# Error and update as one run of matmuls each in a delta-rule attention stage, gram moved between the value products and the error

## The chip, the cores and the metric

The kernel runs on one core of a Trainium2 chip. The metric is the device time of one execution in microseconds, the median of several runs. PE is TensorE, DVE VectorE, ACT ScalarE, POOL GpSimd, and SP the engine that issues the DMAs.

## The reference

Input x has 4 sequences of 4096 rows of 512 numbers; 16 heads of 32. The first layer is a delta rule, step after step in time, and the second a quantised projection:

```python
x = layernorm(x); v = x @ Wv.T; gate = sigmoid(x @ Wg.T); beta = sigmoid(x @ Wb.T)
rk = x by heads, each of norm 1;  wk = rk one row later
for each t:  err = (v_t - wk_t S) * beta_t
             S = S + wk_t err^T
             o_t = (rk_t S) * gate_t
x1  = x  + layernorm(o @ Wo.T)
out = x1 + layernorm(ffn(layernorm(x1)))    # ternary weight, inputs clipped to 128 levels
```

## The kernel before, in words

Three blocks run one after the other: `setup` (weights), `attention` (first layer, some 1850 us) and `feed_forward`. The change touches `attention` alone.

`attention` takes time in tiles of 32 rows of each of the 4 sequences, so 128 partitions and 128 tiles. The recurrence inside a tile is written as a triangular system per head, and tiles are chained by the state. The work is a software pipeline: step j handles tile j in the recurrence, tile j+7 in the value and key products (LAG_V), tile j+6 in the gram matrix (LAG_GRAM), tile j+9 in the turn of x (LAG_TURN), tile j+10 in the normalisation (LAG_XHAT), tile j-3 in the output product (LAG_Y), and so on. All is unrolled: there is no planner, each engine's function `step` has its instructions in an order written by hand, and each engine runs in that order, waiting on semaphores.

One step of PE, in the order before, with the helper that issues it:
- predict (`predict`, L949): the keys times the state, 16 matmuls with 32 weight columns, written as 32 by the hardware (fp32 takes two passes). ACT copies the result into rhs (L611), `turn_back` (L956) transposes it back, and DVE subtracts it from val into rhs (L831).
- value (`value`, L925 through `project`): 12 matmuls of 128x512 into ps_v for tile j+7. WHOLE is 12 and SHARE 3, and `value(first, end)` issues a part of the 12; the parts stand between the other groups.
- gram (L981), behind `gram_ready` (the keys in kbd, loaded by DMA): 16 matmuls, 32 in the hardware.
- error (`solve_error`, L962): 64 matmuls of 32x32 on the 16 small tiles of the array, 128 in the hardware, in two halves of 32 (64). `error_ready` waits for rhs (rhs_done) and for the solved system (tt_done).
- turn of x (L1003, 8) and keys (L1011, 4); ACT copies err (L688), xt and kt.
- output (`output`, L925): 12 matmuls of 128x512 into ps_y for tile j-3, again in parts.
- update (`update`, L1024): 64 matmuls of 32x32, 128 in the hardware, in two halves, behind `update_ready` (err_done, keyb_done). ACT copies the new state (L709), which predict of the next step needs.
- output turn (L1048, 8, behind POOL's olo_done) and gates (`project` with wgb, L925, 12 small ones, behind kt_done). `chain_ready` lets the next predict start.

DVE solves the systems: 30 columns for each pair of tiles (L800 and L808), spread over the steps by `solve(base, j, part)`. In every even step it also turns the systems of a pair (L752) before rhs, and at the end of every odd step it turns the solution back (L816). ss_raw (L838) is the sum of squares for the norms. POOL and ACT do the normalisations, masks and copies.

```python
value(SHARE + 3, 3 * SHARE - 1)
error_ready(base, j)
value(3 * SHARE - 1, 3 * SHARE)
solve_error(0)
last = value(3 * SHARE, 4 * SHARE)
if v_live:
    last.then_inc(s["v_psum"], 1)
last = solve_error(1)
```

Of the kernel before, what the change touches and what calls it, by code (L numbers as in the profile page):

```python
# [272 lines left out]
def attention(nc, io, k):  # L273
    with ExitStack() as ctx:
# [197 lines left out]
        def _(pool):  # L472
# [5 lines left out]
            def step(base, j):  # L478
# [54 lines left out]
                n, l, live = on(base, j, LAG_XHAT)  # L533
                if live:
                    wait(pool, s["xhat_done"], n + 1)
                    wait(pool, s["xhi_done"], n + 1)
                    wait(pool, s["xt_psum"], n - 1)
                    pool.tensor_tensor(x_part[:, l % 2, 1, :], x_hat[:, l % 4, :], x_part[:, l % 2, 0, :],  # L538
                                       ALU.subtract).then_inc(s["xlo_done"], 1)

                n, l, live = on(base, j, LAG_Z)
                if live:
# [8 lines left out]
                    pool.tensor_tensor(kept[:, 1:2], z_mean[:, l % 4, 0:1], kept[:, 0:1], ALU.mult).then_inc(s["z_scale"], 1)  # L551

# [13 lines left out]
                n, l, live = on(base, j, LAG_GRAM)  # L566
                if live:
                    wait(pool, s["gram_done"], n + 1)
                    wait(pool, s["bmask_done"], n + 1)
                    wait(pool, s["sys_done"], times(base, BODY // 2, (j + LAG_GRAM) // 2))  # L570
                    pool.tensor_tensor(m_t[:, :, l % 2, :], gram[:, :, :], b_mask[:, :, :], ALU.mult).then_inc(s["mt_done"], 1)  # L571

                n, l, live = on(base, j, LAG_PART)
                if live:
                    wait(pool, s["ohi_done"], n + 1)
                    wait(pool, s["ot_psum"], n - 1)
                    pool.tensor_tensor(o_part[:, l % 2, 1, :], o_g[:, :], o_part[:, l % 2, 0, :],  # L577
                                       ALU.subtract).then_inc(s["olo_done"], 1)

                n, l, live = on(base, j, 0)  # L580
                if live:
                    wait(pool, s["err_done"], n + 1)
                    wait(pool, s["v_done"], n + 1)
                    wait(pool, s["o_done"], n)
                    pool.tensor_tensor(pred[:, :], val[:, l, :], err[:, l % 2, :], ALU.subtract).then_inc(s["pred_done"], 1)  # L585
# [9 lines left out]
        def _(act):  # L595
            def step(base, j):

                n, l, live = on(base, j, LAG_STATS)
                if live:
                    act.wait_ge(x_loaded[l % 4], quads(base, j, LAG_STATS) * 16 + 16)  # L600
                    wait(act, s["ln_sums"], n)
                    wait(act, s["z_var"], upto(j - 1 + LAG_STATS2 + 1))
                    wait(act, s["ln_mean"], n - 1)
                    nc.scalar.activation(unread["ln", "sum"][:, :], x_in[:, l % 4, :], ACT.Copy,
                                         accum_out=ln_sum[:, l % 2:l % 2 + 1]).then_inc(s["ln_sums"], 1)
# [8 lines left out]
                if live:  # L614
# [5 lines left out]
                                         accum_out=y_var[:, l % 2:l % 2 + 1]).then_inc(s["y_var"], 1)  # L620
                n, l, live = on(base, j, LAG_STATS2)
# [17 lines left out]
                if live:  # L639
# [7 lines left out]
                    wait(act, s["xt_psum"], n - 1)  # L647
# [6 lines left out]
                n, l, live = on(base, j, LAG_PART)  # L654
                if live:
                    wait(act, s["o_done"], n + 1)
                    wait(act, s["ot_psum"], n - 1)
                    nc.scalar.activation(o_part[:, l % 2, 0, :], o_g[:, :], ACT.Copy).then_inc(s["ohi_done"], 1)

                n, l, live = on(base, j, LAG_NORM)  # L660
                if live:
                    wait(act, s["ss_done"], n + 1)
                    wait(act, s["rn0_done"], n)
                    nc.scalar.activation(ss_ln[:, :], ss[:, l % 2, :], ACT.Ln, scale=float(2 ** LN_SHIFT)).then_inc(s["ln_done"], 1)
                    wait(act, s["ln_done"], n + 1)
                    wait(act, s["rn_done"], n - 1)
                    nc.scalar.activation(rn0[:, l % 2, :], ss_ln[:, :], ACT.Exp, scale=-0.5,
# [690 lines left out]
```

## Time and profile before

| what | value |
|---|---|
| median of 3 runs | 2324.56 us (2321.91 to 2326.44) |
| span of the profiled execution | 2313.7 us |
| PE matmul busy | 2084.1 us, 90%, 50216 matmuls and as many weight loads |
| DVE busy | 1992.1 us, 86% |
| ACT busy | 1774.0 us, 77% |
| POOL busy | 1729.0 us, 75% |
| queue "instruction" on q8 | 397 packets, 6.50 MB |

The profile gives the span from the first to the last instruction; it gives no time of its own for the whole execution, and the median of the runs lies 10.9 us above the span. Rows of a timeline give start, duration, engine, line, operation, output and inputs, and in brackets the idle time of the engine before the row with what released it; "issue" is time in which the engine waited for nothing that the profile shows. Matmuls overlap, so the cost of a group is read from its start to the start of the next group. TensorE's granted clock is full speed throughout the loop.

### The profile page before, as it was taken

How to read it: one execution, taken by the hardware profiler on the slowest of the kernel's cores; microseconds unless marked ns; L12 is line 12 of the kernel's file. 1: busy time of each engine (PE TensorE's matmuls, PEld its weight loads, DVE VectorE, ACT ScalarE, POOL GpSimd, SP SyncE). 2: the span in 40 equal slices, each digit the busy share in tenths (PEclk: the TensorE clock that was granted, in tenths of full speed). 3: DMA queues.
4: the chain of work that ended last, by engine and by line, in shares of the span. 5: the costliest groups of instructions: out<-in, count | busy, mean ns of one | idle time of the engine just before them, and what ended most of it. 6: DMA issues, size and time to landing. Idle time of an engine off the chain costs nothing. (4 is left out here: it accounts for less than half of the span.)

```text
span 2313.7 us, 123730 instructions
## 1 busy us (share of the span) xinstructions
PE 2084.1 (90%) x50216; PEld 1316.0 (57%) x50216; DVE 1992.1 (86%) x5810; ACT 1774.0 (77%) x3756; POOL 1729.0 (75%) x3099
## 2 busy tenths in 40 slices
PE   1679999999999999999999999999999987499997
PEld 1346666666666666666655656566666654255554
DVE  5388999999999999999889999899999994588886
ACT  3667888888888888888877878788888744477775
POOL 2668888888888888888888888888888854244443
PEclk7789999999999999999999999999999988799999
DMA  2122333333333333333333333333333222488885
GB/s 86 48 65 80 98 100 98 98 98 95 99 97 99 94 94 95 95 94 94 93 91 93 94 96 91 94 97 96 100 96 99 82 78 67 150 225 229 225 231 129
DMA packets 156632, 247.69 MB, mean 107 GB/s; under 512 B 39544, under 2 KB 39552, under 8 KB 156064
## 3 DMA queue, kind: packets, MB, share of 16 engines
q1 hardware_dynamic: 156064, 239.78, 36.6%
q8 instruction: 397, 6.50, 1.2%
q14 instruction: 171, 1.40, 0.2%
HBM read 104.40 MB, written 67.11 MB: 74 GB/s over the span
## 5 line engine op out<-in xcount | busy, mean ns | idle before, releaser
L800 DVE TENSOR_TENSOR ps_elim<-ps_elim,sys 128x30 f32<-128x30 f32 (+14 forms) x1920 | 543.3, 326 | 0.7
L808 DVE TENSOR_TENSOR sys<-sys,ps_elim 128x30 f32<-128x30 f32 (+14 forms) x1920 | 534.6, 316 | 1.0
L925 PE MATMUL ps_v<-wv,xt 128*128 128x512 f16 x1536 | 435.2, 389 | 39.6 <-DVE rhs L831 16.5
L925 PE MATMUL ps_y<-wo,ot 128*128 128x512 f16 x1536 | 406.1, 386 | 17.3 <-DVE x L852 9.5
L962 PEld LDWEIGHTS ps_chain<-rhs,t_t 32*32 32x32 f32 x16384 | 257.3, 144 | 110.6 <-issue 110.5
L962 PE MATMUL ps_chain<-rhs,t_t 32*32 32x32 f32 x16384 | 286.1, 218 | 13.9 <-issue 8.5
L709 ACT ACTIVATE state<-ps_s 128x512 f32<-128x512 f32 x128 | 76.5, 598 | 265.6 <-PE ps_s L1024 263.6
L1024 PEld LDWEIGHTS ps_s<-err,key_b 32*32 32x32 f32 x16384 | 172.1, 106 | 147.4 <-issue 147.2
L1310 PE MATMUL ps_f<-wq,f_xq 128*128 128x512 f16 x1024 | 242.5, 381 | 6.8 <-DVE f_xq L1276 6.8
L538 POOL TENSOR_TENSOR x_part<-x_hat,x_part 128x512 f16<-128x512 f32 x128 | 148.7, 1162 | 131.6 <-ACT x_hat L645 111.5
L1024 PE MATMUL ps_s<-err,key_b 32*32 32x32 f32 x16384 | 205.5, 195 | 34.2 <-issue 34.2
L925 PEld LDWEIGHTS ps_v<-wv,xt 128*128 128x128 f16 x1536 | 121.0, 99 | 188.4 <-issue 120.5
L925 PEld LDWEIGHTS ps_y<-wo,ot 128*128 128x128 f16 x1536 | 130.2, 98 | 130.3 <-issue 26.3
L831 DVE TENSOR_TENSOR rhs<-val,ps_chain 128x512 f32<-128x512 f32 x128 | 87.4, 682 | 121.1 <-PE ps_chain L956 121.1
L1158 POOL TENSOR_TENSOR f_y_veps<-f_y_var,y_eps 128x1 f32<-128x1 f32 x128 | 53.6, 418 | 184.3 <-ACT f_unread L1191 183.4
L585 POOL TENSOR_TENSOR pred<-val,err 128x512 f32<-128x512 f32 x128 | 163.1, 1274 | 11.3 <-ACT err L688 11.2
L571 POOL TENSOR_TENSOR m_t<-gram,b_mask 128x512 f32<-128x512 f32 x128 | 163.5, 1277 | 5.3 <-ACT gram L674 5.2
L512 POOL TENSOR_TENSOR b_mask<-gates,neg_mask 128x512 f32<-128x512 f32 x128 | 135.5, 1059 | 32.0 <-DVE gates L879 31.9
L1310 PEld LDWEIGHTS ps_f<-wq,f_xq 128*128 128x128 f16 x1024 | 100.2, 98 | 102.0 <-DVE f_xq L1276 7.5
L577 POOL TENSOR_TENSOR o_part<-o_g,o_part 128x512 f16<-128x512 f32 x128 | 148.5, 1160 | 0.0
L949 PE MATMUL ps_chain<-key_bd,state 128*32 128x128 f32 x4096 | 139.9, 277 | 4.3 <-issue 2.8
L714 ACT ACTIVATE ot<-ps_gram 128x1024 f16<-128x1024 f16 x128 | 130.9, 1022 | 16.8 <-PE ps_gram L1048 16.7
(163 smaller groups left out, 5123.6 us busy)
## 6 DMA issues: line engine op xcount, KB each, us to landing
x_in<-in_L_attn_x SPq DMA_DIRECT2D x128, 256.0 KB
kbd<-kt SPq DMA_DIRECT2D x512, 64.0 KB, 2.1
key_bd<-key_t SPq DMA_DIRECT2D x512, 64.0 KB, 2.4
x_res<-in_L_attn_x SPq DMA_DIRECT2D x128, 256.0 KB
x_scratch<-x SPq DMA_DIRECT2D x128, 256.0 KB, 6.3
f_x<-x_scratch SPq DMA_DIRECT2D x32, 1024.0 KB, 7.6
out<-f_res SPq DMA_DIRECT2D x128, 256.0 KB, 3.9
gate<-gates SPq DMA_DIRECT2D x128, 7.9 KB
```

Source lines behind the costliest of these rows:

```text
L512: pool.tensor_tensor(b_mask[:, :, :], beta.unsqueeze(1).to_broadcast([P, C, H]), k["neg_mask"][:, :].unsqueeze(2).to_broadcast([P, C, H]), ...
L538: pool.tensor_tensor(x_part[:, l % 2, 1, :], x_hat[:, l % 4, :], x_part[:, l % 2, 0, :], ALU.subtract).then_inc(s["xlo_done"], 1)
L571: pool.tensor_tensor(m_t[:, :, l % 2, :], gram[:, :, :], b_mask[:, :, :], ALU.mult).then_inc(s["mt_done"], 1)
L577: pool.tensor_tensor(o_part[:, l % 2, 1, :], o_g[:, :], o_part[:, l % 2, 0, :], ALU.subtract).then_inc(s["olo_done"], 1)
L585: pool.tensor_tensor(pred[:, :], val[:, l, :], err[:, l % 2, :], ALU.subtract).then_inc(s["pred_done"], 1)
L800: dve.tensor_tensor(tmp, factors(r, c, first, end)[:, c - first:C - 1 - first, c - first:c - first + 1].to_broadcast(shape), sys[:, r, c:c ...
L808: dve.tensor_tensor(dst, dst, tmp, ALU.add).then_inc(elim_done[r], 1)
L925: last = pe.matmul(out, lhs[:, a, kb, :], weights[:, w, kb, :], start=(i == 0), stop=(i == 3 * KB - 1))
L949: last = pe.matmul(out, state[:, l % 2, HD * h:HD * h + HD], key_bd[:, :, h, :], start=True, stop=True)
L962: last = pe.matmul(ps_chain[q, e], t_t[q, l // 2 % 2, :, l % 2, h], rhs[q, e], start=True, stop=True)
L1024: last = pe.matmul(ps_s[q, e], key_b[q, l, e], err[q, l % 2, e], start=(isinstance(n, int) and n == 0 and h == 0), stop=True, skip_group_c ...
L1310: last = pe.matmul(ps_f[i][:, :], xq[:, r % 2, a, kb, P * i:P * i + P], k["wq"][:, kb, :], start=(m == 0), stop=(m == 2 * KB - 1))
```

## The change

Nothing is computed otherwise; the orders of four engines change.

- PE: all 12 value matmuls are issued before gram (4 before `turn_back`, 8 behind it). `gram_ready` and `error_ready` stand together before gram, so gram comes behind the wait for rhs, and the error's two halves follow it with nothing between. The update's two halves follow each other as well. Five output matmuls stand before the update (three before), then three, the gates, four, and the output turn is last.
- DVE: the reduction ss_raw stands before rhs.
- ACT: the copy of the turned prediction and the square of ps_y come before the sum over x_in; val and gram come before x_part and x_sq; o_part, ss_ln and rn0 come after kt; z before the gates, and ot last.
- POOL: the scale of z comes before x_part; m_t, pred and o_part follow x_part; rn comes after them, and o_g last.

```diff
@@ -823,6 +828,11 @@
                 systems(base, j)
                 diagonal(base, j)
                 multipliers(base, j)
+                m, k_l, k_live = on(base, j, LAG_TURN)
+                if k_live:
+                    wait(dve, s["sq_done"], m + 1)
+                    wait(dve, s["ss_done"], m)
+                    dve.tensor_reduce(ss_raw[:, :], heads(x_sq[:, k_l % 2, :]), AX_X, ALU.add).then_inc(s["ss_sum"], 1)
                 n, l, live = on(base, j, 0)
                 if live:
                     wait(dve, s["pred_psum"], n + 1)
@@ -831,11 +841,6 @@
                     dve.tensor_tensor(rhs[:, :], val[:, l, :], ps_chain[:, :], ALU.subtract).then_inc(s["rhs_done"], 1)
                 solve(base, j, 0)
 
-                m, k_l, k_live = on(base, j, LAG_TURN)
-                if k_live:
-                    wait(dve, s["sq_done"], m + 1)
-                    wait(dve, s["ss_done"], m)
-                    dve.tensor_reduce(ss_raw[:, :], heads(x_sq[:, k_l % 2, :]), AX_X, ALU.add).then_inc(s["ss_sum"], 1)
                 if k_live:
                     wait(dve, s["ss_sum"], m + 1)
                     wait(dve, s["ln_done"], m - 1)
@@ -970,9 +975,11 @@
                     wait(pe, s["xt_done"], upto(v + 2))
                 value(0, SHARE + 1)
                 turn_back()
-                value(SHARE + 1, SHARE + 2)
+                last = value(SHARE + 1, WHOLE)
+                if v_live:
+                    last.then_inc(s["v_psum"], 1)
                 gram_ready(base, j)
-                value(SHARE + 2, SHARE + 3)
+                error_ready(base, j)
                 if m_live:
                     for g in range(KB):
                         for b in range(B):
@@ -980,13 +987,7 @@
                             out = ps_gram[q, :].rearrange("p (i h) -> p h i", h=H)[:, HB * g:HB * g + HB, :]
                             last = pe.matmul(out, kt[:, m_l % 2, g, q], kbd[:, m_l % 2, :, g, q], start=True, stop=True)
                     last.then_inc(s["gram_psum"], 1)
-                value(SHARE + 3, 3 * SHARE - 1)
-                error_ready(base, j)
-                value(3 * SHARE - 1, 3 * SHARE)
                 solve_error(0)
-                last = value(3 * SHARE, 4 * SHARE)
-                if v_live:
-                    last.then_inc(s["v_psum"], 1)
                 last = solve_error(1)
                 if live:
                     last.then_inc(s["err_psum"], 1)
@@ -1028,14 +1029,21 @@
                 if y_live:
                     wait(pe, s["x1_done"], y)
                     wait(pe, s["ot_done"], y + 1)
-                output(0, SHARE - 1)
+                output(0, SHARE + 1)
                 update_ready(base, j)
-                output(SHARE - 1, SHARE)
+                output(SHARE + 1, SHARE + 2)
                 update(0)
-                output(SHARE, 2 * SHARE)
                 last = update(1)
                 if live:
                     last.then_inc(s["s_psum"], 1)
+                output(SHARE + 2, 2 * SHARE + 2)
+
+                if v_live:
+                    wait(pe, s["kt_done"], v + 1)
+                    project(ps_g[:, 0:2 * H], xt[:, v_l % 4], k["wgb"], range(WHOLE)).then_inc(s["g_psum"], 1)
+                last = output(2 * SHARE + 2, WHOLE)
+                if y_live:
+                    last.then_inc(s["y_psum"], 1)
 
                 n, l, live = on(base, j, LAG_OUT)
                 if live:
@@ -1049,16 +1057,8 @@
                                                 o_part[:, l % 2, a, P * kb:P * kb + P], k["ident_half"][:, :])
                     last.then_inc(s["ot_psum"], 1)
 
-                if v_live:
-                    wait(pe, s["kt_done"], v + 1)
-                    project(ps_g[:, 0:2 * H], xt[:, v_l % 4], k["wgb"], range(WHOLE)).then_inc(s["g_psum"], 1)
-
-                output(2 * SHARE, WHOLE - 1)
                 if y_live:
                     chain_ready(base, j + 1)
-                last = output(WHOLE - 1, WHOLE)
-                if y_live:
-                    last.then_inc(s["y_psum"], 1)
             run(step)
 
```

Of ACT's part, the pieces that move between x_hat and err:

```diff
@@ -644,12 +646,50 @@
                     sc = ln_sc[:, l % 2, :]
                     nc.scalar.activation(x_hat[:, l % 4, :], x_in[:, l % 4, :], ACT.Identity,
                                          scale=sc[:, 0:1], bias=sc[:, 1:2]).then_inc(s["xhat_done"], 1)
+                n, l, live = on(base, j, LAG_V)
+                if live:
+                    wait(act, s["v_psum"], n + 1)
+                    wait(act, s["o_done"], n - 7)
+                    wait(act, s["rhs_done"], n - 7)
+                    nc.scalar.activation(val[:, l, :], ps_v[:, :], ACT.Copy).then_inc(s["v_done"], 1)
+
+                n, l, live = on(base, j, LAG_GRAM)
+                if live:
+                    wait(act, s["gram_psum"], n + 1)
+                    wait(act, s["mt_done"], n)
+                    nc.scalar.activation(gram[:, :, :].rearrange("p i h -> p (i h)"), ps_gram[:, :], ACT.Copy).then_inc(s["gram_done"], 1)
+
+                n, l, live = on(base, j, LAG_XHAT)
...
                     wait(act, s["xt_psum"], n - 1)
                     nc.scalar.activation(x_part[:, l % 2, 0, :], x_in[:, l % 4, :], ACT.Identity,
                                          scale=sc[:, 0:1], bias=sc[:, 1:2]).then_inc(s["xhi_done"], 1)
                     wait(act, s["ss_sum"], n - 1)
                     nc.scalar.activation(x_sq[:, l % 2, :], x_in[:, l % 4, :], ACT.Square,
                                          scale=sc[:, 0:1], bias=sc[:, 1:2]).then_inc(s["sq_done"], 1)
+
+                n, l, live = on(base, j, 0)
+                if live:
+                    wait(act, s["err_psum"], n + 1)
+                    wait(act, s["s_psum"], n - 1)
+                    wait(act, s["pred_done"], n - 1)
+                    nc.scalar.activation(err[:, l % 2, :], ps_chain[:, :], ACT.Copy).then_inc(s["err_done"], 1)
+
+                n, l, live = on(base, j, LAG_TURN)
+                if live:
+                    wait(act, s["xt_psum"], n + 1)
+                    wait(act, s["g_psum"], n - 3)
+                    last, most, src = later(l)
+                    nc.scalar.activation(last, src[:, :, 0:1], ACT.Copy)
+                    nc.scalar.activation(most, src[:, :, 1:C], ACT.Copy).then_inc(s["xt_done"], 1)
...
```

PE, one step in the middle of the loop, before (a row is a group of equal matmuls, "x16" their number as written; of the fp32 ones the hardware runs two for each):

```order
L949 MATMUL ps_chain<-key_bd,state 32x128 x16
L925 MATMUL ps_v<-wv,xt 128x512 x4
L956 MATMUL ps_chain<-ident,rhs 128x128 x4
L925 MATMUL ps_v<-wv,xt 128x512 x2
L981 MATMUL ps_gram<-kbd,kt 32x4x32 x16
L925 MATMUL ps_v<-wv,xt 128x512 x3
L962 MATMUL ps_chain<-rhs,t_t 32x32 x32
L925 MATMUL ps_v<-wv,xt 128x512 x3
L962 MATMUL ps_chain<-rhs,t_t 32x32 x32
L1003 MATMUL ps_gram<-ident_half,x_part 128x128 x8
L1011 MATMUL ps_v<-ident,key 128x128 x4
L925 MATMUL ps_y<-wo,ot 128x512 x3
```

The same stretch in the changed kernel, from predict on:

```order
L954 MATMUL ps_chain<-key_bd,state 32x128 x16
L930 MATMUL ps_v<-wv,xt 128x512 x4
L961 MATMUL ps_chain<-ident,rhs 128x128 x4
L930 MATMUL ps_v<-wv,xt 128x512 x8
L988 MATMUL ps_gram<-kbd,kt 32x4x32 x16
L967 MATMUL ps_chain<-rhs,t_t 32x32 x64
L1004 MATMUL ps_gram<-ident_half,x_part 128x128 x8
L1012 MATMUL ps_v<-ident,key 128x128 x4
L930 MATMUL ps_y<-wo,ot 128x512 x5
L1025 MATMUL ps_s<-err,key_b 32x32 x64
```

The error is one row of 64 where it was two of 32 with value matmuls between, gram stands directly before it, and the update is one row.

PE again, the end of the step before the change (from the second half of the update):

```order
L1024 MATMUL ps_s<-err,key_b 32x32 x32
L925 MATMUL ps_y<-wo,ot 128x512 x3
L1024 MATMUL ps_s<-err,key_b 32x32 x32
L1048 MATMUL ps_gram<-ident_half,o_part 128x128 x8
L925 MATMUL ps_v<-wgb,xt 128x32 x12
L925 MATMUL ps_y<-wo,ot 128x512 x6
```

and in the changed kernel, from the update:

```order
L1025 MATMUL ps_s<-err,key_b 32x32 x64
L930 MATMUL ps_y<-wo,ot 128x512 x3
L930 MATMUL ps_v<-wgb,xt 128x32 x12
L930 MATMUL ps_y<-wo,ot 128x512 x4
L1056 MATMUL ps_gram<-ident_half,o_part 128x128 x8
L954 MATMUL ps_chain<-key_bd,state 32x128 x16
```

The output turn (L1048, now L1056) has gone behind the gates and the last four output matmuls, directly before the next predict.

DVE at the start of an even step, before:

```order
L752 STREAM_TRANSPOSE sys<-m_t 128x1024
L759 MEMSET sys 128x32
L779 COPY ps_elim<-sys 128x105
L779 COPY ps_elim<-sys 128x210
L831 TENSOR_TENSOR rhs<-val,ps_chain 128x512
L800 TENSOR_TENSOR ps_elim<-ps_elim,sys 128x240
L800 TENSOR_TENSOR ps_elim<-ps_elim,sys 128x30
...
L808 TENSOR_TENSOR sys<-sys,ps_elim 128x29x2
L838 TENSOR_REDUCE ss_raw<-x_sq 128x16
L843 TENSOR_SCALAR ss<-ss_raw 128x16
```

and now:

```order
L757 STREAM_TRANSPOSE sys<-m_t 128x1024
L764 MEMSET sys 128x32
L784 COPY ps_elim<-sys 128x105
L784 COPY ps_elim<-sys 128x210
L835 TENSOR_REDUCE ss_raw<-x_sq 128x16
L841 TENSOR_TENSOR rhs<-val,ps_chain 128x512
L805 TENSOR_TENSOR ps_elim<-ps_elim,sys 128x240
...
L813 TENSOR_TENSOR sys<-sys,ps_elim 128x29x2
L848 TENSOR_SCALAR ss<-ss_raw 128x16
```

ss_raw (L838, now L835) has moved from behind the first part of the elimination to the place before rhs.

## Rows read from the trace of the kernel before

**Rows 1.** The page, busy time, share of the span and instructions of each engine

```profile
PE 2084.1 (90%) x50216; PEld 1316.0 (57%) x50216; DVE 1992.1 (86%) x5810; ACT 1774.0 (77%) x3756; POOL 1729.0 (75%) x3099
```

**Rows 2.** Timeline of DVE, 386 to 421 us: start, duration, operation, [idle before]

```profile
391.81 0.68 DVE L831 TENSOR_TENSOR rhs<-val,ps_chain 128x512 f32<-128x512 f32 x1
...
404.36 0.69 DVE L831 TENSOR_TENSOR rhs<-val,ps_chain 128x512 f32<-128x512 f32 x1 [1.23 <-PE ps_chain L956]
...
419.70 0.68 DVE L831 TENSOR_TENSOR rhs<-val,ps_chain 128x512 f32<-128x512 f32 x1
```

**Rows 3.** Timeline of PE, predict of two steps, 116 steps apart

```profile
193.17 1.08 PE L949 MATMUL ps_chain<-key_bd,state 128*32 128x128 f32 x32
...
1856.26 1.08 PE L949 MATMUL ps_chain<-key_bd,state 128*32 128x128 f32 x32
```

**Rows 4.** Timeline of PE, 1012 to 1032 us, around two updates

```profile
1012.28 0.63 PE L1011 MATMUL ps_v<-ident,key 128*128 128x128 f32 x4
...
1014.92 0.65 PE L1024 MATMUL ps_s<-err,key_b 32*32 32x32 f32 x52
1016.44 0.31 PE L1024 MATMUL ps_s<-err,key_b 32*32 32x32 f32 x12 [0.86 <-issue]
...
1031.33 0.32 PE L1024 MATMUL ps_s<-err,key_b 32*32 32x32 f32 x13 [1.16 <-issue]
```

**Rows 5.** The page, DMA queue, kind: packets, MB, share of 16 engines

```profile
q8 instruction: 397, 6.50, 1.2%
```

**Rows 6.** Timeline of PE, 1170 to 1182 and 1233 to 1239 us

```profile
1170.70 1.11 PE L962 MATMUL ps_chain<-rhs,t_t 32*32 32x32 f32 x64
...
1173.98 0.30 PE L962 MATMUL ps_chain<-rhs,t_t 32*32 32x32 f32 x3 [0.39 <-issue]
...
1178.95 0.39 PE L1024 MATMUL ps_s<-err,key_b 32*32 32x32 f32 x23 [1.10 <-issue]
...
1234.15 0.31 PE L962 MATMUL ps_chain<-rhs,t_t 32*32 32x32 f32 x7 [0.45 <-issue]
...
1238.61 0.44 PE L1024 MATMUL ps_s<-err,key_b 32*32 32x32 f32 x27 [0.61 <-issue]
```

**Rows 7.** Two stretches: us, busy of PE, PEld, DVE, ACT, POOL, clock, DMA

```profile
200.00:480.00 280.00, 274.41 (x7662) 177.77 (x7656) 261.87 (x848) 239.60 (x520) 248.87 (x441) 1.00 0.34 97
500.00:1130.00 630.00, 597.56 (x16553) 387.35 (x16551) 575.65 (x1848) 522.11 (x1137) 541.13 (x958) 1.00 0.33 96
```

**Rows 8.** Timeline of PE, an even step without a stop on "issue", 390 to 402 us

```profile
390.70 1.08 PE L981 MATMUL ps_gram<-kbd,kt 128*32 128x128 f32 x32
391.72 0.60 PE L925 MATMUL ps_v<-wv,xt 128*128 128x512 f16 x2
392.63 0.38 PE L925 MATMUL ps_v<-wv,xt 128*128 128x512 f16 x1 [0.31 <-DVE rhs L831]
392.94 1.11 PE L962 MATMUL ps_chain<-rhs,t_t 32*32 32x32 f32 x64
393.98 0.82 PE L925 MATMUL ps_v<-wv,xt 128*128 128x512 f16 x3
...
395.78 0.62 PE L1003 MATMUL ps_gram<-ident_half,x_part 128*128 128x128 f16 x8
...
396.68 0.81 PE L925 MATMUL ps_y<-wo,ot 128*128 128x512 f16 x3
...
398.12 0.82 PE L925 MATMUL ps_y<-wo,ot 128*128 128x512 f16 x3
398.88 0.75 PE L1024 MATMUL ps_s<-err,key_b 32*32 32x32 f32 x64
399.62 0.61 PE L1048 MATMUL ps_gram<-ident_half,o_part 128*128 128x128 f16 x8
...
400.36 1.45 PE L925 MATMUL ps_y<-wo,ot 128*128 128x512 f16 x6
401.75 1.08 PE L949 MATMUL ps_chain<-key_bd,state 128*32 128x128 f32 x32
```

More of the change, by code:

```diff
@@ L531, in step @@
                     pool.tensor_tensor(sc[:, 0:1], sc[:, 2:3], k["neg_half"][:, :], ALU.pow).then_inc(s["y_rstd"], 1)
[L533 to L539, printed above, removed]
                 n, l, live = on(base, j, LAG_Z)
@@ L551, in step @@
                     pool.tensor_tensor(kept[:, 1:2], z_mean[:, l % 4, 0:1], kept[:, 0:1], ALU.mult).then_inc(s["z_scale"], 1)
+                n, l, live = on(base, j, LAG_XHAT)
+                if live:
+                    wait(pool, s["xhat_done"], n + 1)
+                    wait(pool, s["xhi_done"], n + 1)
+                    wait(pool, s["xt_psum"], n - 1)
+                    pool.tensor_tensor(x_part[:, l % 2, 1, :], x_hat[:, l % 4, :], x_part[:, l % 2, 0, :],
+                                       ALU.subtract).then_inc(s["xlo_done"], 1)
+                n, l, live = on(base, j, LAG_GRAM)
+                if live:
+                    wait(pool, s["gram_done"], n + 1)
+                    wait(pool, s["bmask_done"], n + 1)
+                    wait(pool, s["sys_done"], times(base, BODY // 2, (j + LAG_GRAM) // 2))
+                    pool.tensor_tensor(m_t[:, :, l % 2, :], gram[:, :, :], b_mask[:, :, :], ALU.mult).then_inc(s["mt_done"], 1)
+                n, l, live = on(base, j, 0)
+                if live:
+                    wait(pool, s["err_done"], n + 1)
+                    wait(pool, s["v_done"], n + 1)
+                    wait(pool, s["o_done"], n)
+                    pool.tensor_tensor(pred[:, :], val[:, l, :], err[:, l % 2, :], ALU.subtract).then_inc(s["pred_done"], 1)
+                n, l, live = on(base, j, LAG_PART)
+                if live:
+                    wait(pool, s["ohi_done"], n + 1)
+                    wait(pool, s["ot_psum"], n - 1)
+                    pool.tensor_tensor(o_part[:, l % 2, 1, :], o_g[:, :], o_part[:, l % 2, 0, :],
+                                       ALU.subtract).then_inc(s["olo_done"], 1)
                 n, l, live = on(base, j, LAG_NORM)
@@ L564, in step @@
                     pool.tensor_tensor(rn[:, l % 2, :], t[:, 2, :], y, ALU.mult).then_inc(s["rn_done"], 1)
[L566 to L578, printed above, removed]
                 n, l, live = on(base, j, 0)
                 if live:
[L582 to L585, printed above, removed]
                     wait(pool, s["pred_done"], n + 1)
@@ L596, in step @@
             def step(base, j):
[L598 to L605, printed above, removed]
                 n, l, live = on(base, j, 0)
@@ L620, in step @@
                                          accum_out=y_var[:, l % 2:l % 2 + 1]).then_inc(s["y_var"], 1)
+                n, l, live = on(base, j, LAG_STATS)
+                if live:
+                    act.wait_ge(x_loaded[l % 4], quads(base, j, LAG_STATS) * 16 + 16)
+                    wait(act, s["ln_sums"], n)
+                    wait(act, s["z_var"], upto(j - 1 + LAG_STATS2 + 1))
+                    wait(act, s["ln_mean"], n - 1)
+                    nc.scalar.activation(unread["ln", "sum"][:, :], x_in[:, l % 4, :], ACT.Copy,
+                                         accum_out=ln_sum[:, l % 2:l % 2 + 1]).then_inc(s["ln_sums"], 1)
                 n, l, live = on(base, j, LAG_STATS2)
```

71 lines of the change are left out of this document (33 added, 38 removed).

## Prediction, made before the changed kernel ran

> **What bounds the kernel now.** I read the engines' busy shares first, then DVE's timeline, then PE's, then the DMA queues. PE is busy 90% and DVE 86% of the span [rows 1]; neither is far from full. DVE waits for rhs in every second step, so the unit is a pair of steps, and DVE's timeline gives its two halves [rows 2]. From rhs of an even step (391.81) to rhs of the odd one (404.36) is 12.55 us, and DVE sat idle 1.23 us before the latter: PE sets this half A. From 404.36 to the next even rhs (419.70) is 15.34 us, and that rhs had no idle time before it: DVE, with its two big transposes, sets this half B. A clean pair is 27.89 us, 13.95 a step. The mean over 116 steps is longer: predict groups start at 193.17 and at 1856.26 [rows 3], 14.34 a step, 28.67 a pair. The missing 0.78 us a pair is what the next two paragraphs explain.
>
> In PE's rows a second kind of stop appears that no engine releases [rows 4]. The second half of the update breaks off after 52 matmuls and goes on at 1016.44 after 0.86 us of "issue"; one step later it goes on at 1031.33 with 13 instead of 12 matmuls left. A step has 380 matmuls (predict 32, value 12, turn back 4, gram 32, error 128, turn 8, keys 4, output 12, update 128, gates 12, output turn 8), as many weight loads and, by the code, some ten waits: about 770 instructions. The page's queue "instruction" on q8 moved 397 packets and 6.50 MB [rows 5], 16.4 KB a packet; with 2 x 50216 matmuls and loads [rows 1] that is 253 of them a packet, 256 with the waits. A step is then three blocks and two instructions, so a block's end comes one matmul earlier in the order each step, which is what 12 and then 13 left over show. I read these stops as PE waiting for its own instructions.
>
> The prices: two late blocks in a row resume at 1173.98 and 1178.95, and at 1234.15 and 1238.61 [rows 6], some 126 matmuls apart: a block takes 4.5 to 5.0 us, mean 4.7, after a late one. After a punctual one it takes less: the block that ends late at 1016.44 began 126 matmuls earlier, at the start of the keys' transposes at 1012.28 [rows 4], 4.2 us; the one that ends late at 1173.98 began just behind 1170.70 [rows 6], 3.3 us. Where instructions are long, nobody notices: in 200 to 480 us PE is busy 274.4 of 280 us, in 500 to 1130 us only 597.6 of 630 [rows 7], 2% idle against 5%, with the same work in each step and block ends at other places. The Trainium skill says the opposite (Runtime: NRT & Kernel Launch, section Instruction fetch mechanics): fetching in blocks of 256 instructions is hidden, because instructions issue slower than they are fetched. The rows above speak against it here. By the page these stops would be something else and need not grow; that outcome is the first rival.
>
> **The change, part by part.**
>
> *Fewer changes of matmul form.* Six output matmuls before predict take 1.39 us (400.36 to 401.75), three before an update 0.76 (398.12 to 398.88) [rows 8]: 0.21 each and 0.13 for going over to small tiles. Leaving them shows in no row by itself; I take 0.1 for a change either way, bounds 0 and 0.13. Before, a step enters and leaves small tiles six times; now three times (predict; gram and error together; update), with one change from gram's form to error's between. Five changes fewer are 0.5 us of PE a step (0.2 to 0.65). By that term alone the step would shrink from 14.34 to 13.84, 58 us in 116 steps, if PE were the only bound. The Trainium skill (TensorEngine Tiling (Array Packing), section Key Properties) has the rule behind it, that a change of tiling mode drains the engine; it speaks for the change, and what speaks against is below.
>
> *Half A.* PE's way from the start of the error (392.94) to the odd rhs (404.36) is 11.42 us [rows 2, 8]. Out of it go three value matmuls (0.64, now ahead of the gate for rhs) and four form changes (0.4); into it comes gram, which now stands behind that gate: 1.02 us (390.70 to 391.72) [rows 8]. That is 11.4. The value matmul and its wait between the end of rhs (391.81 + 0.68) and the error, 0.45, shrink to 0.1. A becomes 0.68 + 0.1 + 11.4 = 12.2, 0.35 less than 12.55.
>
> *Half B.* DVE's own instructions stay, so 15.34 stays. The reduction of squares (ss_raw) goes ahead of rhs in every step; what it adds before one rhs it takes away before the next, so it leaves each half as long as it was and costs nothing. If that cover were gone it would cost its own place in A, at most the idle 1.23. PE's way through half B is now some 13.0 us (11.42 from the error on, and 2.1 for two value matmuls, gram and three value matmuls before it, less 0.5), so late blocks of up to 2.3 us in B cost nothing; before it was 1.8.
>
> *Blocks of instructions.* This term decides. From the start of gram to the end of the update PE took 8.4 us (390.70 to 399.62, less half a us of wait for rhs) [rows 8] for 312 matmuls: 3.45 us per 128, one block. Now the same stretch holds gram 1.0, error 2.0 (two times 1.04 less one form change), turn and keys 0.9 (395.78 to 396.68), five output matmuls 1.2, update 1.4 (two times 0.74 less 0.1): 6.5 us for 305 matmuls, 2.7 us a block. The number of instructions stays. A block after a punctual one needs 3.3 to 4.2, so it is late by 0.6 to 1.5, and after a late one 4.7, so late by 2.0. Three block ends fall into the stretch in (305 - 256) / 128, 38% of the steps: together 0.6 and 2.0, 2.6. In the others two do: about 0.9, and some 0.5 for the block that runs on into the long matmuls behind. The mean is 0.38 x 2.6 + 0.62 x 1.4 = 1.85 us a step, against 0.78 now.
>
> *Waits on the other engines.* ACT copies val and gram ahead of x_part and x_sq, whose readers come a step later. The copy of err ends the chain gram, its copy, two passes, while PE spends 3.0 us on gram and error: even, and one more output matmul (0.2) stands before the update: 0. The state copy has output, gates and output turn as cover. POOL's o_part after pred is awaited only at the step's end. SP's queue is not touched; its loads of kbd and key_bd start when ACT's kt and DVE's key_t are done, as before. I take 0 for all of these, bounds -0.2 and +0.3 a pair.
>
> **The sum.** A: 12.2 + 1.85 = 14.05; B: 15.34. The pair is 29.4, before 28.67: +0.7, +0.35 a step, and with 116 steps +40 us. The loop's ends and the second stage stay. The span of the profiled execution would go from 2313.7 to some 2353; the median of the runs (2324.56) lies 11 us above that span, so it goes to about 2363, and I say 2362. If late time stays at 0.78 the pair is 28.3, 58 pairs are -20 us: 2304. If the stretch costs 3.5 us (first block 4.2) in 38% and 2.0 in the rest, the mean is 2.6 and the worst steps overflow B's cover of 2.3 by some 0.2 a pair: 30.3, +1.65 a pair, 2420; I cut that end at 2405.
>
> **Rivals.**
> 1. *The stops do not grow.* For: in 200 to 480 us there are nearly none, although PE is as full. Against: the remainder that grows by one, and stops of the same kind inside the error [rows 6]. Then -20 us, 2304, faster; it decides if late time stays under 0.78 + 0.35 us a step, what half A gains otherwise. Chance 0.20.
> 2. *DVE covers it.* If most late blocks fall into half B, late time in A of 1.15 gives 12.2 + 1.15 + 15.34 = 28.7 a pair, 2326, the same. Against: a block's end moves by one matmul a step, so both halves see it. Chance 0.05.
> 3. *The gate for rhs before gram.* In even steps rhs ends late; now gram, its copy, m_t and err queue behind it, not the error alone. If the copy of err comes 0.25 late each step a pair costs another 0.5: +29 on the forecast, 2391. For: two ACT passes stand between gram and err. Against: the two chains come out even. Chance 0.10.
>
> **How the numbers follow.** The forecast, slower by late blocks, has 0.65. About 0.2% (4.6 us) is what a measurement can tell from no change. Faster is rival 1, 0.20; the same is rival 2, 0.05; slower are the forecast and rival 3, 0.75. The range reaches from just under rival 1, 2298, to near the upper bound of late blocks, 2405.
>
> **What would show it.** Right: idle time of PE on "issue" in error, update, output and gates of over 1.5 us a step in most steps, its place moving by one matmul a step; no value matmul between the halves of the error and PE's busy time lower; clean pairs of some 27.5 us where they occur; more idle time of DVE before the odd rhs than 1.23 us. Wrong: pairs of 27.5 to 28.3 throughout (rival 1); idle time of PE that ACT's err releases (rival 3); "issue" stops whose place does not move.

## The result, and the profile after

Four runs of the changed kernel have a median of 2363.45 us (2355.82 to 2369.17), the kernel before 2325.5 beside them: a ratio of 1.0164, with a 95% interval of 1.0134 to 1.0194. It is slower by 1.6%, some 38 us. Forecast were 2362 us and "slower". The profiled execution took 2355.82 us, its span is 2354.1.

In this run and in all later ones the span lies 1.7 to 1.8 us below the time of the same execution. So a profile is one execution of several, and not always a typical one: the profiled one of before (span 2313.7) was some 9 us faster than the median of its kernel, this one 7.6 us faster. Traces are compared below with that in mind; what an edit is worth is read from the medians.

The page of the changed kernel, busy time of each engine, then the costliest groups that answer to the update, the error and gram (line, engine, operation, tiles, count | busy, mean ns | idle before, releaser):

```profile
PE 2036.5 (87%) x50216; PEld 1361.3 (58%) x50216; DVE 1955.2 (83%) x5810; ACT 1804.7 (77%) x3756; POOL 1724.8 (73%) x3099
...
L967 PE MATMUL ps_chain<-rhs,t_t 32*32 32x32 f32 x16384 | 268.8, 218 | 32.0 <-issue 26.7
...
L1025 PE MATMUL ps_s<-err,key_b 32*32 32x32 f32 x16384 | 195.7, 195 | 65.0 <-issue 64.4
...
L988 PE MATMUL ps_gram<-kbd,kt 128*32 128x128 f32 x4096 | 138.4, 275 | 42.9 <-DVE rhs L841 41.1
```

Against [rows 1] PE is busy 47.6 us less, with the same 50216 matmuls, and yet the kernel is slower. The last lines name two waits of PE that outweigh it: idle time on "issue" in update and error, and a wait for DVE's rhs ahead of gram.

Timeline of PE, predict of the two steps that [rows 3] shows of before:

```profile
188.87 1.12 PE L954 MATMUL ps_chain<-key_bd,state 128*32 128x128 f32 x32
...
1891.95 1.08 PE L954 MATMUL ps_chain<-key_bd,state 128*32 128x128 f32 x32
```

That is 1703.1 us for 116 steps, 14.68 a step against 14.34: 40 us more. All of the loss is in the loop.

Timeline of PE, two steps in a row, around the stops:

```profile
1018.71 0.22 PE L1004 MATMUL ps_gram<-ident_half,x_part 128*128 128x128 f16 x1 [0.42 <-issue]
...
1022.75 0.31 PE L1025 MATMUL ps_s<-err,key_b 32*32 32x32 f32 x11 [0.96 <-issue]
...
1033.85 0.27 PE L1004 MATMUL ps_gram<-ident_half,x_part 128*128 128x128 f16 x2 [0.66 <-issue]
...
1038.17 0.31 PE L1025 MATMUL ps_s<-err,key_b 32*32 32x32 f32 x12 [1.23 <-issue]
```

These are the stops of [rows 4]: 11 matmuls of the update left over, then 12; 1 transpose of the turn left over, then 2. The place moves by one matmul a step, and now there are two stops in a step. Between 193 and 1856 us PE's idle time on "issue" sums up to 107.2 us in the table of waits, against 47.1 before.

Timeline of DVE, rhs of an even step, of the odd one behind it and of the next even one, with the residual sum (L857) between:

```profile
303.24 0.68 DVE L841 TENSOR_TENSOR rhs<-val,ps_chain 128x512 f32<-128x512 f32 x1
...
315.69 0.69 DVE L841 TENSOR_TENSOR rhs<-val,ps_chain 128x512 f32<-128x512 f32 x1 [1.40 <-PE ps_chain L961]
320.15 0.75 DVE L857 SCALAR_TENSOR_TENSOR x<-ps_y,y_sc,x_res 128x512 f32<-128x512 f32 x1 [1.64 <-DMA x_res<-in_L_attn_x]
...
332.19 0.68 DVE L841 TENSOR_TENSOR rhs<-val,ps_chain 128x512 f32<-128x512 f32 x1
```

Half A is 12.45 us here (forecast without stops: 12.2), half B 16.50 (forecast: 15.34, as in [rows 2]). In this pair B has grown because DVE sat 1.64 us waiting for the load of x_res, for which it never waited this long before. Over the 58 pairs from step 4 on, by the starts of rhs, the mean of A went from 13.23 to 13.64 and that of B from 15.45 to 15.75.

Over the loop another wait of DVE grew more. Its `gates` row (the reciprocal near the end of a step) waits for ACT's g_den, which follows the gate matmuls of PE. Tables of waits from 193 to 1856 us, before, changed, and then a_locked and a_locked_late, two kernels of the next section that differ only in where blocks of PE's instructions end:

```profile
DVE gates L879 <- ACT g_den L724: 20.2, 28, 2.0
...
DVE gates L884 <- ACT g_den L732: 76.0, 69, 2.7
...
DVE gates L884 <- ACT g_den L732: 8.4, 19, 0.7
...
DVE gates L884 <- ACT g_den L732: 157.1, 107, 3.2
```

So late blocks reach DVE by this path as well as by rhs. Summed by halves over the 58 pairs, DVE's idle time went from 1.91 to 2.53 us a pair in A and from 0.13 to 0.90 in B. In A nearly all of the growth is g_den (17.2 to 49.4 us in 58 pairs); in B it is g_den (1.0 to 26.6) and, less, the row that reads x_res (6.5 to 24.2).

DVE's own work, on the other hand, became shorter: 1955.2 us busy against 1992.1, and by halves, idle time taken out, 11.11 us against 11.32 in A and 14.85 against 15.32 in B. Most of it is ss, which stood directly behind ss_raw and now stands behind a part of the elimination (groups of DVE, before and changed: busy, mean ns | idle before):

```profile
L843 DVE TENSOR_SCALAR ss<-ss_raw 128x16 f32<-128x16 f32 x128 | 50.0, 390 | 4.8 <-POOL rn_t L559 0.5
...
L848 DVE TENSOR_SCALAR ss<-ss_raw 128x16 f32<-128x16 f32 x128 | 22.7, 177 | 1.7 <-POOL rn_t L579 1.5
```

Why ss is the shorter there was not tried by itself.

Two timelines of the same moment: PE, and stretches of 3.4 us (us, PE busy, granted clock as a share of 2.4 GHz, DMA share, GB/s):

```profile
333.02 1.08 PE L988 MATMUL ps_gram<-kbd,kt 128*32 128x128 f32 x32 [2.28 <-DVE rhs L841]
334.03 2.04 PE L967 MATMUL ps_chain<-rhs,t_t 32*32 32x32 f32 x128
336.00 1.03 PE L1004 MATMUL ps_gram<-ident_half,x_part 128*128 128x128 f16 x8
336.83 1.05 PE L1012 MATMUL ps_v<-ident,key 128*128 128x128 f32 x4
```

```profile
327.50:330.90 3.40, 3.24 (x20) 1.00 0.50 110
330.90:334.30 3.40, 1.28 (x52) 1.00 0.24 90
334.30:337.70 3.40, 3.40 (x137) 0.50 0.27 90
```

PE waits 2.28 us ahead of gram, and 1.3 us behind that wait the clock falls to 1.2 GHz for 3.4 us. The error takes no longer in it, the transposes do: 1.03 and 1.05 us, where the clock is full 0.62 and 0.63. There are 15 such falls between 200 and 1850 us; before, there is none.

### The profile page after: what moved, and what is told of

It reads as the page before. It is cut to its first block and busy times, and to the rows that moved or that the text cites. A ratio compares the mean times of both kernels' runs of the same rounds, so it can differ in the third digit from the quotient of the medians.

```text
span 2354.1 us, 123730 instructions
## 1 busy us (share of the span) xinstructions
PE 2036.5 (87%) x50216; PEld 1361.3 (58%) x50216; DVE 1955.2 (83%) x5810; ACT 1804.7 (77%) x3756; POOL 1724.8 (73%) x3099
## 5 line engine op out<-in xcount | busy, mean ns | idle before, releaser
L930 PE MATMUL ps_y<-wo,ot 128*128 128x512 f16 x1536 | 413.7, 394 | 21.0 <-DVE x L857 11.2
L930 PE MATMUL ps_v<-wv,xt 128*128 128x512 f16 x1536 | 385.9, 390 | 6.5 <-ACT xt L685 4.2
L967 PE MATMUL ps_chain<-rhs,t_t 32*32 32x32 f32 x16384 | 268.8, 218 | 32.0 <-issue 26.7
L967 PEld LDWEIGHTS ps_chain<-rhs,t_t 32*32 32x32 f32 x16384 | 250.6, 145 | 61.3 <-issue 61.2
L1025 PE MATMUL ps_s<-err,key_b 32*32 32x32 f32 x16384 | 195.7, 195 | 65.0 <-issue 64.4
L930 PEld LDWEIGHTS ps_v<-wv,xt 128*128 128x128 f16 x1536 | 142.8, 100 | 164.4 <-issue 39.6
L988 PE MATMUL ps_gram<-kbd,kt 128*32 128x128 f32 x4096 | 138.4, 275 | 42.9 <-DVE rhs L841 41.1
L988 PEld LDWEIGHTS ps_gram<-kbd,kt 128*32 128x32 f32 x4096 | 105.8, 109 | 99.8 <-issue 99.8
```

Source lines behind the costliest of these rows:

```text
L930: last = pe.matmul(out, lhs[:, a, kb, :], weights[:, w, kb, :], start=(i == 0), stop=(i == 3 * KB - 1))
L967: last = pe.matmul(ps_chain[q, e], t_t[q, l // 2 % 2, :, l % 2, h], rhs[q, e], start=True, stop=True)
L988: last = pe.matmul(out, kt[:, m_l % 2, g, q], kbd[:, m_l % 2, :, g, q], start=True, stop=True)
L1025: last = pe.matmul(ps_s[q, e], key_b[q, l, e], err[q, l % 2, e], start=(isinstance(n, int) and n == 0 and h == 0), stop=True, skip_group_c ...
```

## The experiments

The open questions were: are the stops on "issue" really late blocks of instructions; are they the loss, or is it the wait for rhs ahead of gram (rival 3); and what stands behind them.

**Stops at fixed places.** A step is 770 instructions, three blocks and two: the traces of before and of the changed kernel have exactly 770 records of PE (matmuls, weight loads and its sequencer's) from one predict to the next. Two of PE's waits in it repeat what PE has already waited for, with the same value. Without them a step is 768 in the trace, and a block's end stays where it is.

```
-                    wait(pe, s["xt_done"], upto(v + 2))
+                    if not on(base, j - 1, LAG_OUT)[2]:
+                        wait(pe, s["xt_done"], upto(v + 2))
...
                     wait(pe, s["x1_done"], y)
-                    wait(pe, s["ot_done"], y + 1)
+                    if not on(base, j, LAG_GRAM)[2]:
+                        wait(pe, s["ot_done"], y + 1)
```

For the two "late" kernels this stands ahead of PE's first step as well; the traces have 1190 records of PE ahead of the first predict where the others have 1030, so 320 waits are 160 instructions:

```
+            for i in range(320):
+                pe.wait_ge(s["state_done"], 1)
```

> The kernel before, with two waits a step left out on PE that repeat a wait PE has already passed, so that a step is 768 instructions, three blocks of 256. If the stops are late blocks, a block's end stays at the places of steps 4 to 11 (in predict, in the error, in the update), where the trace of before shows 13.75 us a step and hardly a stop: 13.8 to 13.95 a step for 116 steps against 14.34, some 2262 to 2280 us, below both kernels. Rival, the stops are not tied to the count of instructions: they stay, two short waits fewer, 2315 to 2325.

> As b_locked, but 320 waits that are met at once stand ahead of PE's first step (160 instructions), which puts the block ends at the places of steps 80 to 92 (gram, middle of the error, middle of the update), for good. If the stops are late blocks: 14.65 us a step as the trace of before shows there, 2360 us, some 90 above b_locked with the same work. Rival: the same time as b_locked.

> The changed kernel with the same two repeated waits left out, block ends as in b_locked. If late blocks are the loss, nearly no stops: 13.65 us a step as in its own steps 4 to 11, up to 14.3 if what steps 12 to 20 show is the new wait for rhs ahead of gram: 2250 to 2320, I take 2296. Against b_locked it tells what the change does without late blocks: my first rival's arithmetic says 20 us less than b_locked; if the gate for rhs ahead of gram costs more than the form changes give, it is slower than b_locked. Rival (stops not tied to instructions): 2355.

> The changed kernel, locked as b_locked_late. If late blocks are the loss: 15.4 us a step as in its steps 76 to 90, against 14.68 on average, some 2445 us, and its distance to a_locked (150) is larger than that of the two before (90). Rival: the same time as a_locked.

Measured: b_locked 2311.1 us, ratio 0.9961 (0.9931 to 0.9992); b_locked_late 2355.8, 1.0140 (1.0121 to 1.0158); a_locked 2326.5, 0.9999 (0.9984 to 1.0014); a_locked_late 2427.4, 1.0443 (1.0423 to 1.0463).

Each pair has the same work in the same order on every engine and differs only by waits that are met at once, ahead of the loop; 45 us lie between the two of before and 101 between the two of the change. Two steps in a row of a_locked_late, timeline of PE:

```profile
871.43 0.42 PE L969 MATMUL ps_chain<-rhs,t_t 32*32 32x32 f32 x14 [0.58 <-issue]
...
876.24 0.46 PE L1028 MATMUL ps_s<-err,key_b 32*32 32x32 f32 x33 [1.38 <-issue]
...
890.64 0.46 PE L1028 MATMUL ps_s<-err,key_b 32*32 32x32 f32 x33 [1.11 <-issue]
```

33 matmuls are left over in both steps: the stop no longer moves. In a_locked and b_locked the stops on "issue" are gone (0.0 and 0.5 us between 193 and 1850). So the stops follow the count of PE's instructions, and the order of the change pays more for them.

The sizes were missed in both good cases: 2262 to 2280 was expected for b_locked, and a_locked was to be faster than it, not 15 us slower. In b_locked 47 us of stops are gone and only some 9 are won by the ratio (2 to 16 by its interval). Its table of waits from 193 to 1856 us (engine, line waited for: us, times, longest), PE first and then SP:

```profile
PE ps_v L925 <- DMA kbd<-kt: 56.0, 67, 1.4
...
PE ps_y L925 <- DMA key_bd<-key_t: 10.5, 34, 0.7
...
SPq L456 <- ACT kt L702: 7.8, 7, 3.1
SPq L440 <- DVE gates L879: 1.0, 3, 0.5
```

PE now waits for the loads of kbd and key_bd, for which it waited 4.1 and 4.7 us before, and SP, which issues them, waits for other engines 8.8 us in 1663. It has its next transfer to issue nearly all the time. Half A fell from 13.23 to 12.95, half B rose from 15.45 to 15.77. That the sum does not fall is the choice of executions: the profiled one of b_locked was 9 us slower than its median, the profiled one of before some 9 faster. In a_locked PE waits at the gate for rhs ahead of gram, and else it is the same in other places:

```profile
PE ps_gram L989 <- DVE rhs L841: 100.2, 56, 2.6
PE ps_chain L954 <- DMA key_bd<-key_t: 30.8, 54, 1.1
...
DVE x L857 <- DMA x_res<-in_L_attn_x: 63.9, 41, 2.4
DVE x L857 <- issue: 23.0, 30, 2.3
```

The row "issue" is very probably the same wait: its 30 cases start 6.3 to 7.2 us after SP issued x_res, the 41 named ones 6.1 to 7.6. Both together are 86.9 us in a_locked, 26.5 in b_locked, 29.1 in the changed kernel and 7.8 in before.

Like with like, without late blocks on either side, the change is still some 0.4% slower (0.9999 against 0.9961, 15 us; the two intervals just touch).

**SP's queue, and the wait for rhs.** In the "act" kernels the load of x_in is issued by ACT from step 0 on, with the same waits; in the "gate" kernels the wait for rhs stands behind gram:

```
-                gram_ready(base, j)
-                error_ready(base, j)
+                gram_ready(base, j)
                 if m_live:
...
+                error_ready(base, j)
                 solve_error(0)
```

> b_locked showed no late block, yet 14.35 us a step: PE waits there for the kbd loads (56 us in 67 waits) and SP's queue hardly ever waits for an engine (7.8 us in 1664). Theory: once late blocks are gone, SP's queue of 13 transfers a step is the bound. Here x_in is loaded from ACT's queue from step 0 on, nothing else differs from b_locked. By the theory the waits for kbd and x_res go and a step falls to the 13.8 to 14.0 that half A and half B allow: 2265 to 2285 us. Rival: the transfers themselves are late (DMA engines or memory), whatever the queue: 2305 to 2320.

> The changed kernel, locked, x_in loaded from ACT's queue. a_locked waits 63.9 us for x_res on DVE and 30.8 for key_bd on PE. If SP's queue is the cause both go: 2326 becomes 2280 to 2300. What then stays above b_locked_act is the price of the order itself, the gate for rhs ahead of gram. Rival: 2320 to 2330.

> The changed kernel, locked, with the wait for rhs put between gram and the error, not ahead of gram. a_locked has PE waiting 100 us ahead of gram in 56 even steps for DVE's rhs. Theory: gram's 1.0 us stands on the way from the even rhs to the odd one, so moving it ahead of the wait gives up to 1.0 us a pair, 58 us, cut by SP's queue which is at 14.3 us a step: 2290 to 2315. Rival, the wait for rhs only moves and the pair is set by DVE or SP alone: 2326 as a_locked.

> All three: locked, x_in from ACT's queue, the wait for rhs behind gram. If late blocks, SP's queue and the gate are the three losses of the change, what is left is the gain of fewer changes of form: half A 0.35 us or more below b_locked_act's, 20 us or more: 2240 to 2265. Rival: the form changes give nothing and it equals b_locked_act.

Measured: b_locked_act 2309.1, 0.9938 (0.9913 to 0.9963); a_locked_act 2307.7, 0.9939 (0.9913 to 0.9966); a_locked_gate 2309.2, 0.9924 (0.9894 to 0.9954); a_locked_gate_act 2272.9, 0.9778 (0.9734 to 0.9822).

The theory of SP's queue holds in half. PE's wait for kbd falls from 56.0 to 5.1 us in b_locked_act and the one for key_bd from 30.8 to 5.1 in a_locked_act, but DVE's for x_res stays, 26.3 and 54.9 (with "issue" 28.0, and 109.3 where a_locked had 86.9), and single ones become longer:

```profile
DVE x L859 <- DMA x_res<-in_L_attn_x: 26.3, 17, 3.9
```

That is b_locked_act; the longest was 1.2 us in b_locked. So b_locked gains too little to be told from nothing (the intervals overlap), not the 26 to 46 us expected, while a_locked gains 0.6%. Where DVE waits for it in b_locked_act, it goes on 8.5 us after the issue of x_res on average, in b_locked 6.8 us after. So at least that part lies behind the issue and not in SP's order; what holds the transfer up was not tried.

The gate was worth 0.75%, 17 us, as expected. Each of the two edits alone brings the locked kernel to 2308 or 2309, both together to 2273. The tables of waits show how one takes what the other frees. In a_locked PE waits 100.2 us for rhs and 30.8 for key_bd. With the gate edit these are 43.0 and 50.2; with the x_in edit 86.5 and 5.1; with both 40.7 and 2.0. That kernel is below both kernels of the case, 2.2% under before. Its page and the predict of the same two steps:

```profile
PE 2026.4 (89%) x50216; PEld 1353.9 (60%) x50216; DVE 1968.6 (87%) x5810; ACT 1799.6 (79%) x3756; POOL 1723.1 (76%) x3099
```

```profile
191.08 1.40 PE L961 MATMUL ps_chain<-key_bd,state 128*32 128x128 f32 x32
...
1811.70 1.08 PE L961 MATMUL ps_chain<-key_bd,state 128*32 128x128 f32 x32
```

13.97 a step: half A 12.09, half B 15.86. DVE's idle time ahead of rhs is 15.2 us in the 58 pairs, against 92.3 in before: PE hardly sets half A any more. DVE's wait at the row that reads x_res is still 88.6 us ("issue" counted in), the largest of DVE's that is left.

**The change itself, taken apart.** a_gate is the changed kernel with the gate edit alone, a_gate_act with the x_in edit too; both keep 770 instructions. The other two cross the kernels: PE's whole block from one, the rest of the program from the other.

> The changed kernel with only the wait for rhs moved from ahead of gram to ahead of the error; block ends move by one matmul a step as they did. In the locked kernels this was worth 17 us (2326 to 2309). Theory: late blocks are the larger part of the loss and stay, so about as much is won: 2340 to 2352, still slower than before. If the gate were the main cause of the loss, it would fall to 2325 or below.

> As a_locked_gate_act (2273), but not locked: the two repeated waits are back and a block's end moves by one matmul a step. Late blocks alone make the difference: the change lost 37 us between its locked and its plain form, so 2305 to 2320 here. If locking gave nothing beyond two waits fewer, 2275 to 2285.

> PE's order of the changed kernel, DVE, ACT and POOL in the order of before. If the loss lies in PE's order alone (my term of 0 for the other engines), 2355 to 2370 as the changed kernel. If the other engines' new order is what makes the change bearable, slower: 2380 and more. If it is part of the loss, faster than 2355.

> PE's order of before, DVE, ACT and POOL in the order of the change. If the other engines' order costs nothing: 2320 to 2332. If it costs, more; with late blocks as in before in any case.

Measured: a_gate 2323.7, 1.0003 (0.9977 to 1.0029); a_gate_act 2312.9, 0.9948 (0.9921 to 0.9974); pe_after_rest_before 2508.7, 1.0801 (1.0758 to 1.0844); pe_before_rest_after 2424.9, 1.0443 (1.0403 to 1.0483).

a_gate was expected at 2340 to 2352 and came out as before: one wait, moved by 32 matmuls, takes back the whole loss. Its timelines of PE and of DVE:

```profile
306.95 1.08 PE L987 MATMUL ps_gram<-kbd,kt 128*32 128x128 f32 x32
308.83 2.02 PE L967 MATMUL ps_chain<-rhs,t_t 32*32 32x32 f32 x128 [0.80 <-DVE rhs L841]
```

```profile
308.01 0.68 DVE L841 TENSOR_TENSOR rhs<-val,ps_chain 128x512 f32<-128x512 f32 x1
...
319.52 0.69 DVE L841 TENSOR_TENSOR rhs<-val,ps_chain 128x512 f32<-128x512 f32 x1
```

Gram runs while DVE computes rhs, and this half A is 11.51 us, 0.94 less than the 12.45 above, which is gram's 1.02. Half B grew there, and took back a part: by the means over the 58 pairs A is 12.89 and B 16.03. The falls of the clock are nearly as many (13), so they are not the difference. The stops on "issue" are fewer, 77.8 us against 107.2, still more than the 47.1 of before.

a_gate_act against a_locked_gate_act puts the price of late blocks at 1.7%, 40 us, in the middle of what was expected.

The crossed kernels are slower than either, by 8.0% and 4.4%, far outside what was expected of them (2355 to 2370, and 2320 to 2332). In pe_after_rest_before the table of PE's waits has among its first places:

```profile
PE ps_chain L956 <- ACT rhs L611: 113.4, 103, 1.3
...
PE ps_v L925 <- ACT g_exp L720: 27.5, 98, 0.3
```

ACT comes late with the copy that turning back needs, in nearly every step. Ahead of it in ACT's old order stand the copy of ot and four more instructions (g_exp, g_den, z and the sum over x_in), and PE's new order turns the output last in the step: ACT waits 198.0 us for it in 103 steps, and the four come behind that wait. In pe_before_rest_after ACT waits 173.5 us for val in 110 steps, since PE finishes val late in its old order while ACT asks for it early.

## Why the prediction was right, and where its reasons were not

*The number.* A pair of 29.4 us was forecast; by the starts of rhs it is 13.64 + 15.75 = 29.39, against 28.69 before. The mechanism that was to decide, late blocks, is there and is a cause. That the sum is right to the hundredth is chance: half A was to be 14.05 and half B 15.34, and the two errors cancel. The step from a span to a median, taken as 11 us, is no property of the kernel either: it was 9.4 this time, because both profiled executions were among the fast ones.

*Form changes.* Forecast 0.5 us of PE a step, bounds 0.2 to 0.65. PE is busy 47.6 us less in 128 steps, 0.37 a step. Right within the bounds, a little large; the falls of the clock take some of it back.

*Half A, late time of 1.85 us.* This is the term that was mis-sized most. Stops on "issue" went from 47.1 to 107.2 us, more than doubled, and their place moves by one matmul a step: kind and direction are right. But they are 0.92 us a step, and over 1.5 in 31 of 116 steps, not in most. The starting value was off as well: the 0.78 that the prediction sets beside 1.85 is what a *pair* lacked, and the trace of before has 0.41 us of stops a step. In half A alone the stops are 0.96 us where 1.85 was forecast. The rest of A is longer than forecast by as much as half of that error: a_locked, which has no stops, has a mean of 12.69 where 12.2 was forecast, and 12.69 + 0.96 is the 13.64 measured.

That late blocks are a loss is shown by the locked pairs (45 and 101 us) and by a_locked, which has none and is 1.65% faster than the changed kernel. The rule of the Trainium skill that the prediction weighed (Runtime: NRT & Kernel Launch, section Instruction fetch mechanics), by which fetching in blocks of 256 is hidden, did not hold in this kernel: 160 instructions that do nothing, ahead of the loop, cost 4.4% in it.

*The gate for rhs.* The prediction put gram's 1.02 us into half A, and that price is right: the shortest halves A are 12.11 us in the changed kernel and 11.11 in a_gate, where gram stands ahead of the gate. What failed is the conclusion. The 1.02 was netted against what leaves half A, and "slower by late blocks" stood as the one cause. The runs show that the gate alone is worth 1.6% in the changed kernel, 37 us, and 0.75% where late blocks are gone. So the loss has two causes, each of which is enough for nearly all of it: without late blocks the change is at 0.9999, without the gate at 1.0003, without both at 0.9924. They don't add up. One reason could be that a wait ahead of gram pushes gram, error, turn and update into one dense run, where the blocks are then later. It fits the 77.8 us of stops against 107.2; it was not tried by itself.

*Half B stays at 15.34.* Wrong by 0.4, and in two directions. DVE's own part of B was to stay and fell from 15.32 to 14.85, mostly by the shorter ss: moving ss_raw was to leave each half as it was. Its idle time in B was to stay near nothing and went from 0.13 to 0.90. The prediction took rhs as the only place where DVE waits for PE and gave late blocks in B 2.3 us of cover. But DVE's gates wait for ACT's g_den at the end of every step, and it came late with the blocks. No part of the prediction looked at x_res either: "SP's queue is not touched" is true of its order, and missed that SP had little time to spare. Before, it waited for other engines 62.6 us of 1663. Among the kernels that load x_in from SP, the shorter half A is the longer half B: 13.23 and 15.45 before, 12.69 and 16.23 in a_locked, 12.06 and 16.48 in a_locked_gate.

*Waits on the other engines, taken as 0.* This holds for the chain it was worked out for: in the changed kernel PE never waits for ACT's copy of err. It does not hold for g_den. And the crossed kernels show that the order of the other engines had to change with PE's: half of the change would have cost some 100 or 185 us.

*Rivals.* Rival 1, stops that don't grow (2304), is refuted. Rival 2, DVE's cover, too: the stops lie in even steps as in odd ones (0.96 and 0.89 us a step), and B grew. Rival 3 pointed at the right wait, but with another mechanism: its cost was to come through a late copy of err, and its sign, idle time of PE that ACT's err releases, is in no row of the changed kernel's waits. What the gate costs is gram's own place in half A.

*What would show it.* Clean pairs of some 27.5 us do occur, though seldom: 6 of the 58 are under 28 us, 27.62 and 27.63 among them. The pair in the rows above (28.95) is not one of them, since x_res is late in it. DVE's idle time ahead of rhs is 89.8 us against 92.3, not more. That pointed away from PE's late time in half A as the whole of the loss.

## What to carry to other kernels

Where several bounds lie within a few per cent of each other (here PE's order, its instruction blocks, DVE's chain and the loads from SP's queue), removing one shows little until the next is gone too: two edits worth 0.6 and 0.75% alone brought 2.2% together. When stages are merged, look first at which wait moved up with them, and put each wait directly ahead of the first instruction that needs it. Where engines' orders are written by hand, expect them to fit each other: here each half of the change alone was worse than either kernel. And where a loop's step is close to a whole number of instruction blocks, making it exactly that, with the ends in long instructions, takes the stops away.

## What the runs showed that was not expected

- **A kernel's time depends on where its loop begins in the count of instructions.** 160 instructions ahead of the loop, met at once, move the changed kernel from 2326.5 to 2427.4 us, and the kernel before from 2311.1 to 2355.8.
- **The granted clock falls to 1.2 GHz for 3.4 us at a time inside a busy loop.** In the changed kernel each fall begins 1.2 to 3.9 us after the start of a stop of PE of 0.7 to 2.6 us. There are 15 in the changed kernel, 19 in a_locked, 25 in a_locked_late, 13 in a_gate, none in before, b_locked and b_locked_late. What it costs depends on the form: the error in 32 x 32 tiles took 2.04 us against 2.02, the transposes in full tiles 0.83 us more together. At that price 15 falls are some 12 us, an estimate.
- **Thirteen transfers a step leave SP hardly any time to spare.** Most issues take 0.5 to 0.7 us, but the four of key_bd took 7 us, of which the first took 5.2, where the trace shows no engine that they waited for. The kernel before, timeline of SP:

```profile
391.11 7.05 SPq L448 DMA_DIRECT2D key_bd<-key_t  x4
398.20 2.98 SPq L456 DMA_DIRECT2D kbd<-kt  x4
401.23 0.62 SPq L461 DMA_DIRECT2D x_res<-in_L_attn_x  x1
```
